# First experts of a small transformer tower: the second weights held in the array, 416 columns of hidden values moving

## Chip, cores and metric

The program runs on one core of a Trainium2 chip. The metric is the device time of one execution in microseconds (us), smaller is better. Times of the kernel before are the median of three runs and one execution taken with the hardware profiler. The engines are PE (matrix products), DVE (vector), ACT (activations), POOL (GpSimd) and SP (it issues the DMAs).

## What is computed

Four blocks of a transformer on 64 short sequences of 26 tokens, 1664 tokens of 192 values, all in fp32. The change is in the feed-forward part of the first block, where every token goes through all 32 experts:

```python
def _L0_ffn_ref(x, gate_w, gate_b, w1, b1, w2, b2):
    C = 192; E = 32; H = 4 * C
    gates = jax.nn.softmax(x @ gate_w + gate_b, axis=-1)
    h = jax.nn.gelu(jnp.einsum('btc,ech->bteh', x, w1) + b1, approximate=False)
    y = jnp.einsum('bteh,ehc->btec', h, w2) + b2
    out = jnp.einsum('bte,btec->btc', gates, y)
    return out
```

The result is added to the tokens `h` (`h = h + ffn(layernorm(h))`), and the next block begins with a layer norm of the sum.

## The kernel before

The 1664 tokens are 13 tiles of 128 (`TILES`), in four blocks of 3, 3, 3 and 4 tiles (`BLOCKS`, L33), so 384, 384, 384 and 512 tokens. The hidden size 768 is six chunks of 128 (`HC`). Products run in the fp32r type. To keep precision each operand is divided into a high part (the value cast to fp32r) and a low part (the value less its high part), and a product is made of several.

**Up products.** `up(e, j, k)` (L845) makes the six hidden chunks of block k: `five` (L590) issues five products a chunk, with 128 columns of the first weights stationary and the block's 384 or 512 normalised tokens moving. The chunk has channels down and tokens along. It lands in one of four PSUM banks (4 to 7). ACT applies GELU into one of three `hid` buffers (L905), DVE casts it to `hid_hi` (L936) and subtracts to get `hid_lo` (L939).

**Down products.** `down(e, j, k)` (L858) takes the tiles of a block one by one. The stationary operand is the hidden tile, 128 channels by 128 tokens. Moving is `w2[j]`, whose row holds 192 columns of high and 192 of low part, and each chunk has two products:

```python
nc.tensor.matmul(o[:, 0:2 * D], hid_hi[k % 2][:, m, c], w2[j][:, m, :],
                 start=m == 0, stop=False)
ins = nc.tensor.matmul(o[:, 0:D], hid_lo[k % 2][:, m, c], w2[j][:, m, 0:D],
                       start=False, stop=m == HC - 1)
```

The result has tokens down and the 192 outputs along (high part of the weights in the first 192 columns of the bank, low part in the second). `gather` (L954) on DVE multiplies each half with the tile's gate, a value per token and so per partition, and adds it to `h_tok` in one operation (L962, L968). Four banks (0 to 3) take the tiles in turn. The second biases, weighted with the gates, are 13 products of the turned gates (`gate_t`, 32 x 1664) with the biases (L842), added by L921.

**Order.** Each engine has its own order written out, tied by semaphores. On PE an expert is `up(0), up(1), down(0), up(2), down(1), up(3), down(2), down(3)`; on DVE it is `split(0), split(1), gather(0), split(2), gather(1), split(3), gather(2), gather(3)`. Two experts are the body of a hardware loop. In expert 0, `logits` comes ahead, the turning of the gates stands after `up(0)`, the second biases after `up(1)`. In the last expert DVE adds statistics (L389) and means (L393) of each finished tile, which the next phase's root needs all of.

**Weights.** SP loads an expert's 1344 KB into `raw[j]` two experts ahead (L808). POOL divides them in `split_weights` (L756): the high parts after half of the previous expert's splits, the low parts (L768, L771) after all of its 24 splits. PE waits for them at the head of an expert.

## Time and profile before

| | us |
|---|---|
| median of 3 runs | 2989.89 |
| lowest and highest | 2987.41, 2991.16 |
| the profiled execution | 2989.68 |
| its span in the trace | 2987.9 |

In 40 slices of the span, each digit the busy share in tenths (PEclk is the granted clock of PE in tenths of full speed):

```profile
PE   8889999999999999999999788797988889957678
PEld 7679999999999999999999687676566789945557
DVE  3867777777777777777777788523569567778876
ACT  2433233233333233333233344311555333334433
POOL 1312211211211211211211211021213101122550
PEclk9889999999999999999999899798989889978888
```

The first experts are the slices from the third to the twenty-second. PE's busy time is the union of its products' intervals, which overlap: a product's duration is longer than its distance to the next.

### The profile page before, as it was taken

The numbers are of one execution on the slowest core, as the hardware profiler recorded it, in microseconds if no ns is written. First come the engines' busy times: TensorE is split into PE (matmuls) and PEld (weight loads), VectorE is DVE, ScalarE is ACT, GpSimd is POOL, SyncE is SP. The second block draws the span as 40 slices with busy tenths as digits, with TensorE's granted clock in tenths as the row PEclk, the third lists the DMA queues.
The fourth block names the chain that finished last, engine by engine and source line by source line (L and its number), as shares of the span: only waits on it lengthen the run. The fifth ranks groups of instructions, "written<-read, shape, count | busy, mean of one in ns | idle before, by whom it ended". The sixth has DMA issues, their size and how long they took to land. (4 is left out here: it accounts for less than half of the span.)

```text
span 2987.9 us, 57872 instructions
## 1 busy us (share of the span) xinstructions
PE 2719.2 (91%) x20693; PEld 2465.2 (83%) x20693; DVE 2088.5 (70%) x5299; ACT 1061.3 (36%) x2060; POOL 620.7 (21%) x807
## 2 busy tenths in 40 slices
PE   8889999999999999999999788797988889957678
PEld 7679999999999999999999687676566789945557
DVE  3867777777777777777777788523569567778876
ACT  2433233233333233333233344311555333334433
POOL 1312211211211211211211211021213101122550
PEclk9889999999999999999999899798989889978888
DMA  3001001011011011010001000085000100000000
GB/s 141 20 38 38 21 36 37 19 37 37 19 37 37 19 37 37 19 37 37 19 19 40 2 2 2 17 251 155 1 12 4 54 19 19 1 11 17 25 20 18
DMA packets 24466, 105.65 MB, mean 35 GB/s; under 512 B 4455, under 2 KB 9463, under 8 KB 19086
## 3 DMA queue, kind: packets, MB, share of 16 engines
q1 hardware_dynamic: 22654, 99.62, 9.6%
q0 software_dynamic: 1584, 3.30, 0.3%
q8 instruction: 105, 1.72, 0.2%
q14 instruction: 123, 1.01, 0.1%
HBM read 98.32 MB, written 6.64 MB: 35 GB/s over the span
## 5 line engine op out<-in xcount | busy, mean ns | idle before, releaser
L905 ACT ACTIVATE hid<-bank,dat 128x384 f32<-128x384 f32 (+1 forms) x912 | 554.4, 608 | 1144.1 <-PE bank L595 1032.3
L870 PE MATMUL bank<-w,hid_hi 128*128 128x384 f32 x2964 | 858.5, 361 | 2.2 <-DVE y_tok L921 1.6
L872 PE MATMUL bank<-w,hid_lo 128*128 128x192 f32 x2964 | 745.5, 252 | 0.0
L872 PEld LDWEIGHTS bank<-w,hid_lo 128*128 128x128 f32 x2964 | 570.7, 193 | 1.7
L870 PEld LDWEIGHTS bank<-w,hid_hi 128*128 128x128 f32 x2964 | 561.3, 189 | 5.7 <-issue 4.1
L939 DVE TENSOR_TENSOR hid_lo<-hid,hid_hi 128x384 fp32r<-128x384 f32 (+1 forms) x912 | 539.8, 592 | 31.5
L936 DVE CAST hid_hi<-hid 128x384 fp32r<-128x384 f32 (+1 forms) x912 | 341.0, 374 | 126.6 <-ACT hid L905 125.2
L962 DVE SCALAR_TENSOR_TENSOR h_tok<-bank,gate,h_tok 128x192 f32<-128x192 f32 x416 | 173.5, 417 | 246.8 <-PE bank L872 243.4
L595 PE MATMUL bank<-xa_hi,w_hi 128*128 128x384 f32 (+1 forms) x912 | 324.5, 356 | 8.3 <-DVE w_lo L748 5.1
L595 PE MATMUL bank<-xa_lo,w_hi 128*128 128x384 f32 (+1 forms) x912 | 323.0, 354 | 0.0
L595 PE MATMUL bank<-xb,w_lo 128*128 128x384 f32 (+1 forms) x912 | 322.4, 353 | 0.0
L595 PE MATMUL bank<-xa_hi,w_lo 128*128 128x384 f32 (+1 forms) x912 | 321.7, 353 | 0.0
L595 PE MATMUL bank<-xb,w_hi 128*128 128x384 f32 (+1 forms) x912 | 320.2, 351 | 0.0
L768 POOL TENSOR_TENSOR w_lo<-raw,w_hi 128x1536 fp32r<-128x1536 f32 x36 | 125.6, 3490 | 675.6 <-DVE hid_lo L939 675.6
L1632 POOL COPY n_tok<-p_x 32x312 f32<-32x312 f32 (+1 forms) x192 | 94.3, 491 | 476.0 <-DVE p_x L2198 330.5
L595 PEld LDWEIGHTS bank<-xa_hi,w_hi 128*128 128x128 f32 x912 | 172.6, 189 | 18.3 <-issue 5.7
L968 DVE SCALAR_TENSOR_TENSOR h_tok<-bank,gate,h_tok 128x192 f32<-128x192 f32 x416 | 173.7, 418 | 14.5
L595 PEld LDWEIGHTS bank<-xb,w_hi 128*128 128x128 f32 x912 | 172.6, 189 | 10.6
L763 POOL CAST w_hi<-raw 128x1536 fp32r<-128x1536 f32 x36 | 52.8, 1466 | 618.1 <-DVE hid_lo L939 564.6
L595 PEld LDWEIGHTS bank<-xa_hi,w_lo 128*128 128x128 f32 x912 | 172.5, 189 | 9.9
L595 PEld LDWEIGHTS bank<-xb,w_lo 128*128 128x128 f32 x912 | 172.3, 189 | 9.8
L595 PEld LDWEIGHTS bank<-xa_lo,w_hi 128*128 128x128 f32 x912 | 172.9, 190 | 8.5
(359 smaller groups left out, 4286.2 us busy)
## 6 DMA issues: line engine op xcount, KB each, us to landing
raw<-in_L_exp SPq DMA_DIRECT2D x36, 1344.0 KB, 5.7
w_e<-in_L_exp SPq DMA_DIRECT2D x20, 576.0 KB, 4.0
w_e<-in_L_exp SPq DMA_DIRECT2D x20, 384.0 KB
pix<-in_pixels SPq DMA_DIRECT2D x6, 832.0 KB, 10.4
w_e<-in_L_exp SPq DMA_DIRECT2D x20, 195.0 KB
raw<-in_L_mlp SPq DMA_DIRECT2D x2, 1344.0 KB, 5.6
wp_raw<-in_L_att SPq DMA_DIRECT2D x1, 2304.0 KB, 8.3
route_rows<-in_rows_clear SPq DMA_DIRECT2D x1, 2000.0 KB, 23.0
```

The source lines that it names most:

```text
L595: ins = nc.tensor.matmul(o, l, r, start=start and n == 0, stop=stop and n == 4)
L763: nc.gpsimd.tensor_copy(w1_hi[j][:, :, :], r1).then_inc(s["w_split"].sem, 1)
L768: nc.gpsimd.tensor_tensor(w1_lo[j][:, :, :], r1, w1_hi[j][:, :, :].bitcast(F32), ALU.subtract).then_inc(s["w_split"].sem, 1)
L870: nc.tensor.matmul(o[:, 0:2 * D], hid_hi[k % 2][:, m, c], w2[j][:, m, :], start=m == 0, stop=False)
L872: ins = nc.tensor.matmul(o[:, 0:D], hid_lo[k % 2][:, m, c], w2[j][:, m, 0:D], start=False, stop=m == HC - 1)
L905: nc.scalar.activation(hid[(6 * k + m) % 3][:, 0:128 * nt], bank[4 + (6 * k + m) % 4][:, 0:128 * nt], func, bias=bias).then_inc(s["h_act"] ...
L936: nc.vector.tensor_copy(hid_hi[k % 2][:, m, 0:w], h).then_inc(s["dve_step"].sem, 1)
L939: nc.vector.tensor_tensor(hid_lo[k % 2][:, m, 0:w], h, hid_hi[k % 2][:, m, 0:w].bitcast(F32), ALU.subtract).then_inc(s["h_split"].sem, 1)
L962: nc.vector.scalar_tensor_tensor(res[:, t, :], o[:, 0:D], g, res[:, t, :], ALU.mult, ALU.add).then_inc(s["dve_step"].sem, 1)
L968: nc.vector.scalar_tensor_tensor(res[:, t, :], o[:, D:2 * D], g, res[:, t, :], ALU.mult, ALU.add).then_inc(s["y_used"].sem, 1)
L1632: nc.gpsimd.tensor_copy(p_bd[t % 2][r, :, SLOT * im:SLOT * im + SLOT], p_x[t % 2][r, 0:H, 0:SLOT]).then_inc(s["bd_low"].sem, 1)
```

## The change

For the first experts alone `turned_experts_phase` stands in place of `experts_phase`.

- Tokens are taken in four equal spans of 416 (`SPANS`), for the up products, ACT and the splits too.
- The down products have the second weights stationary and `hid_hi` or `hid_lo` of a span moving, 416 columns. Part 0 makes outputs 0 to 127 with three products a chunk (high x high, high x low, low x high). Part 1 makes outputs 128 to 191 with two: its stationary operand `both` holds 64 columns of high and 64 of low part, so that the upper 64 partitions of the result are the share of the weights' low part. So 18 + 12 = 30 products a span.
- The result has outputs down and tokens along. The gate is then a value per column. The 32 x 1664 turned gates are written to DRAM, and for each expert and span one row of 416 is read back into all 128 partitions of `gate_b`. DVE multiplies with it into `y_new` and adds `y_new` to the sums `y_sum`, which lie in `y_tok` (part 0) and `n_tok` (part 1): four operations a span.
- The second biases are 8 products of 416 columns, copied into the sums.
- In the last expert PE turns the finished sums back, tile by tile: a transpose of part 0 and a product of part 1 with `fold`, a 128 x 64 table that adds partitions p and p + 64. DVE adds the result to `h_tok` and takes statistics and means.
- POOL's low part of the second weights is two operations (768 and 384 elements) in place of one of 1152, its high part likewise.
- SP's loop over the experts is written out, with the gate rows' DMAs between the weights'. On PE and DVE the last two experts stand outside the loop (on DVE they did before).

The diff, cut to its core:

```diff
+SPANS = [(416 * k, 416) for k in range(4)]
+DONE = [(0, 3), (3, 3), (6, 3), (9, 4)]
...
+        y_new = [sb(f"y_new{j}", [128, 416], scope=ex) for j in range(2)]
...
+        gate_b = sb("gate_b", [128, TOK], scope=ex)
...
+        def turned_w2(j):
+            flat = w2[j][:, :, :].rearrange("p c n -> p (c n)")
+            return [flat[:, HC * 128 * y:HC * 128 * (y + 1)].rearrange("p (c n) -> p c n", c=HC) for y in range(3)]
+        def split_turned(pool, b, e, j, i, before_low=None):
...
+            a_hi, a_lo, both = turned_w2(j)
+            nc.gpsimd.tensor_copy(w1_hi[j][:, :, :], r1).then_inc(s["w_split"].sem, 1)
+            nc.gpsimd.tensor_copy(a_hi, ra).then_inc(s["w_split"].sem, 1)
+            nc.gpsimd.tensor_copy(both[:, :, 0:DB], rb).then_inc(s["w_split"].sem, 1)
+            if before_low:
+                before_low()
+            pool.wait_ge(s["w_split"].sem, b["w_split"] + 6 * e + 1)
+            nc.gpsimd.tensor_tensor(w1_lo[j][:, :, :], r1, w1_hi[j][:, :, :].bitcast(F32),
+                                    ALU.subtract).then_inc(s["w_split"].sem, 1)
+            pool.wait_ge(s["w_split"].sem, b["w_split"] + 6 * e + 3)
+            nc.gpsimd.tensor_tensor(a_lo, ra, a_hi.bitcast(F32), ALU.subtract).then_inc(s["w_split"].sem, 1)
+            nc.gpsimd.tensor_tensor(both[:, :, DB:2 * DB], rb, both[:, :, 0:DB].bitcast(F32),
+                                    ALU.subtract).then_inc(s["w_split"].sem, 1)
...
+            def sync(sp):
+                def gate_rows(e, k):
+                    c0, n = SPANS[k]
+                    line = gates_d[e:e + 1, c0:c0 + n]
+                    sp.dma_start(gate_b[:, c0:c0 + n], bass.AP(line.tensor, line.offset, [[0, 128], [1, n]]))                        .then_inc(gate_in[k], 16)
+                sp.wait_ge(s["t_used"].sem, gating["kept"])
+                sp.dma_start(gates_d[:, :], gate_t[0:E, :]).then_inc(gate_out, 16)
+                sp.wait_ge(gate_out, 16)
+                for k in range(4):
+                    gate_rows(0, k)
+                for e in range(E):
+                    if e + 2 < E:
+                        sp.wait_ge(s["w_split"].sem, b["w_split"] + 6 * (e + 1))
+                        sp.dma_start(raw[e % 2][:, :], dram[e + 2]).then_inc(w_in[e % 2].sem, 16)
+                    for k in range(4):
+                        if e + 1 < E:
+                            sp.wait_ge(s["y_used"].sem, b["y_used"] + down_unit(e, k) + 2)
+                            gate_rows(e + 1, k)
...
+                def second_biases():
+                    gating["tensor"][2](pe)
+                    w = dat[0:E, DATA_COLS[b2_col]]
+                    for u in range(8):
+                        c0, n = SPANS[u // 2]
+                        if u >= 4:
+                            pe.wait_ge(s["y_used"].sem, b["y_used"] + u - 3)
+                        nc.tensor.matmul(bank[u % 4][:, 0:n], w[:, 128 * (u % 2):128 * (u % 2) + 128],
+                                         gate_t[0:E, c0:c0 + n], start=True, stop=True).then_inc(s["y_full"].sem, 1)
...
+                def down(e, j, k):
+                    n = SPANS[k][1]
+                    a_hi, a_lo, both = turned_w2(j)
+                    u = down_unit(e, k)
+                    pe.wait_ge(s["h_split"].sem, b["h_split"] + 24 * e + 6 * k + 6)
+                    for part in range(2):
+                        pe.wait_ge(s["y_used"].sem, b["y_used"] + u + part - 3)
+                        o = bank[(down_unit(0, k) + part if not is_last(e) else u + part) % 4][:, 0:n]
+                        for m in range(HC):
+                            hi, lo = hid_hi[k % 2][:, m, 0:n], hid_lo[k % 2][:, m, 0:n]
+                            steps = ((a_hi, hi), (a_hi, lo), (a_lo, hi)) if part == 0 else ((both, hi), (both, lo))
+                            for y, (w, x) in enumerate(steps):
+                                ins = nc.tensor.matmul(o, w[:, m, :], x, start=m == 0 and y == 0,
+                                                       stop=m == HC - 1 and y == len(steps) - 1)
+                        ins.then_inc(s["y_full"].sem, 1)
+                def back(k):
+                    t0, nt = DONE[k]
+                    pe.wait_ge(s["dve_step"].sem, b["dve_step"] + added(E - 1, k))
+                    for part in range(2):
+                        u = back_unit(k) + part
+                        pe.wait_ge(s["y_used"].sem, b["y_used"] + u - 3)
+                        for y, t in enumerate(range(t0 + 2 * part, min(t0 + 2 * part + 2, t0 + nt))):
+                            o, c = bank[u % 4][:, D * y:D * y + D], slice(128 * t, 128 * t + 128)
+                            nc.tensor.transpose(o[:, 0:DA], y_sum[0][:, c], shp[:, SHAPE_COLS["ident"]])
+                            ins = nc.tensor.matmul(o[:, DA:D], y_sum[1][:, c], shp[:, SHAPE_COLS["fold"]], start=True,
+                                                   stop=True)
+                        ins.then_inc(s["y_full"].sem, 1)
+                def body(e, j, i):
+                    pe.wait_ge(s["w_split"].sem, b["w_split"] + 6 * (e + 1) - (2 if is_first(e) else 0))
+                    up(e, j, 0)
+                    if is_first(e):
+                        gating["tensor"][1](pe)
+                    for k in range(1, 4):
+                        up(e, j, k)
+                        if is_first(e) and k == 1:
+                            second_biases()
+                            pe.wait_ge(s["w_split"].sem, b["w_split"] + 6)
+                        down(e, j, k - 1)
+                        if is_last(e) and k > 1:
+                            back(k - 2)
+                    down(e, j, 3)
+                    if is_last(e):
+                        back(2)
+                        back(3)
+                over_experts(pe, body, 1)
...
+                def keep_second_biases():
+                    for u in range(8):
+                        c0, n = SPANS[u // 2]
+                        dve.wait_ge(s["y_full"].sem, b["y_full"] + u + 1)
+                        nc.vector.tensor_copy(y_sum[u % 2][:, c0:c0 + n], bank[u % 4][:, 0:n]).then_inc(s["y_used"].sem, 1)
...
+                def gather(e, j, k):
+                    c0, n = SPANS[k]
+                    c = slice(c0, c0 + n)
+                    u = down_unit(e, k)
+                    dve.wait_ge(gate_in[k], 16 * (e + 1))
+                    if not (is_first(e) and k == 0):
+                        dve.wait_ge(s["dve_step"].sem, b["dve_step"] + (added(e, k - 1) if k else STEPS * e))
+                    for part in range(2):
+                        dve.wait_ge(s["y_full"].sem, b["y_full"] + u + part + 1)
+                        o = bank[(down_unit(0, k) + part if not is_last(e) else u + part) % 4][:, 0:n]
+                        nc.vector.tensor_tensor(y_new[part][:, 0:n], o, gate_b[:, c], ALU.mult)                            .then_inc(s["y_used"].sem, 1)
+                    for part in range(2):
+                        dve.wait_ge(s["y_used"].sem, b["y_used"] + u + part + 1)
+                        nc.vector.tensor_tensor(y_sum[part][:, c], y_sum[part][:, c], y_new[part][:, 0:n], ALU.add)                            .then_inc(s["dve_step"].sem, 1)
+                def add_back(k):
+                    t0, nt = DONE[k]
+                    for part in range(2):
+                        u = back_unit(k) + part
+                        m = min(2, nt - 2 * part)
+                        t = t0 + 2 * part
+                        dve.wait_ge(s["y_full"].sem, b["y_full"] + u + 1)
+                        nc.vector.tensor_tensor(res[:, t:t + m, :], bank[u % 4][:, 0:D * m].rearrange("p (t d) -> p t d", d=D),
+                                                res[:, t:t + m, :], ALU.add).then_inc(s["y_used"].sem, 1)
+                        for y in range(t, t + m):
+                            statistics(dve, res, y, s["y_used"].sem, b["y_used"] + u + 1)
+                    for y in range(t0, t0 + nt):
+                        mean_of(dve, y, before)
+                def body(e, j, i):
+                    split(e, j, 0)
+                    for k in range(1, 4):
+                        split(e, j, k)
+                        if is_first(e) and k == 1:
+                            keep_second_biases()
+                        gather(e, j, k - 1)
+                        if is_last(e) and k > 1:
+                            add_back(k - 2)
+                    gather(e, j, 3)
+                    if is_last(e):
+                        add_back(2)
+                        add_back(3)
+                over_experts(dve, body, 1)
...
-        experts_phase(32, a["L0_exp"], "L0_b1", "L0_b2", h_tok, ACT.Gelu, w, g, stats_of=h_tok)
+        turned_experts_phase(32, a["L0_exp"], "L0_b1", "L0_b2", h_tok, ACT.Gelu, w, g)
...
+    o[p, SHAPE_COLS.lo("fold") + p % 64] = 1
...
-    col("L0_b2", g["L0_ffn_b2"])
+    col("L0_b2", np.pad(g["L0_ffn_b2"], ((0, 0), (0, 256 - D))))
...
-        "L0_exp": expert_pack(g["L0_ffn_w1"], g["L0_ffn_w2"]),
+        "L0_exp": turned_pack(g["L0_ffn_w1"], g["L0_ffn_w2"]),
```

On PE, in the first expert: the second biases and the first down products before. `w_0` is the second weights' buffer 0, `dat` holds the biases and `feat` the turned gates.

```order
L595 MATMUL bank<-xb,w_lo 128x384
L842 MATMUL bank<-dat,feat 128x192 x13
L870 MATMUL bank<-w_0,hid_hi 128x384
L872 MATMUL bank<-w_0,hid_lo 128x192
L870 MATMUL bank<-w_0,hid_hi 128x384
```

And the same place now, with the first five of the 30 down products of the span:

```order
L602 MATMUL bank<-xb,w_lo 128x416
L892 MATMUL bank<-feat,dat 128x416 x8
L919 MATMUL bank<-hid_hi,w_0 128x416
L919 MATMUL bank<-hid_lo,w_0 128x416
L919 MATMUL bank<-hid_hi,w_0 128x416 x2
L919 MATMUL bank<-hid_lo,w_0 128x416
```

The 36 products of three tiles, of 384 and 192 columns in turn, have become 30 of 416 for a span.

On DVE, the gather behind the second split of the first expert, before:

```order
L939 TENSOR_TENSOR hid_lo<-hid,hid_hi 128x384
L921 TENSOR_TENSOR h_tok<-bank,h_tok 128x192 x13
L962 SCALAR_TENSOR_TENSOR h_tok<-bank,gate,h_tok 128x192
L968 SCALAR_TENSOR_TENSOR h_tok<-bank,gate,h_tok 128x192
L962 SCALAR_TENSOR_TENSOR h_tok<-bank,gate,h_tok 128x192
```

And now:

```order
L981 COPY n_tok<-bank 128x416
L1008 TENSOR_TENSOR y_new<-bank,gate_b 128x416 x2
L1011 TENSOR_TENSOR y_tok<-y_tok,y_new 128x416
L1011 TENSOR_TENSOR n_tok<-n_tok,y_new 128x416
L992 CAST hid_hi<-hid 128x416
L994 TENSOR_TENSOR hid_lo<-hid,hid_hi 128x416
```

Six operations that read a bank and one tile are now two that read a bank and the gates, and two that read two tiles of SBUF.

On PE, the last expert, behind the third span's up products and the second's down products:

```order
L919 MATMUL bank<-hid_lo,w_1 128x416
L932 MATMUL bank<-shp,y_tok 128x128
L933 MATMUL bank<-shp,n_tok 128x64
L932 MATMUL bank<-shp,y_tok 128x128
L933 MATMUL bank<-shp,n_tok 128x64
L932 MATMUL bank<-shp,y_tok 128x128
L933 MATMUL bank<-shp,n_tok 128x64
L602 MATMUL bank<-xa_hi,w_hi 128x416
```

These turns of three tiles stand there once more a span later, and seven tiles are turned after the last down product.

## Rows read from the trace of the kernel before

**Rows 1.** The page's part 1, busy time by engine.
```profile
PE 2719.2 (91%) x20693; PEld 2465.2 (83%) x20693; DVE 2088.5 (70%) x5299; ACT 1061.3 (36%) x2060; POOL 620.7 (21%) x807
```

**Rows 2.** Windows: start:end length, busy us (instructions) by engine, PEclk, DMA share, GB/s.
```profile
240.00:1580.00 1340.00, 1340.00 (x8238) 1299.72 (x8237) 974.11 (x2213) 438.08 (x720) 256.61 (x119) 1.00 0.08 30
197.80:204.80 7.00, 5.93 (x27) 5.14 (x27) 5.73 (x18) 0.58 (x1) 2.55 (x2) 0.78 0.00 0
```

**Rows 3.** PE's timeline, two experts: start us, us, line, output<-inputs.
```profile
1003.86 0.36 PE L595 MATMUL bank<-xa_hi,w_hi 128*128 128x384 f32 x1
...
1009.12 0.34 PE L595 MATMUL bank<-xa_hi,w_hi 128*128 128x384 f32 x1
...
1029.82 0.42 PE L595 MATMUL bank<-xa_hi,w_hi 128*128 128x512 f32 x1
...
1036.80 0.34 PE L870 MATMUL bank<-w,hid_hi 128*128 128x384 f32 x1
...
1048.64 0.25 PE L872 MATMUL bank<-w,hid_lo 128*128 128x192 f32 x1
1048.72 0.36 PE L595 MATMUL bank<-xa_hi,w_hi 128*128 128x384 f32 x1
```

**Rows 4.** PE's timeline, query and key projections of the first attention.
```profile
60.15 0.35 PE L595 MATMUL bank<-xa_lo,wp_hi 128*96 128x416 f32 x1
...
61.66 0.35 PE L595 MATMUL bank<-xb,wp_lo 128*96 128x416 f32 x1
```

**Rows 5.** PE's timeline: turns, clock-keeping products, second biases of the first experts.
```profile
171.11 0.27 PE L447 MATMUL bank<-shp,n_tok 128*128 128x128 f32 x1
171.22 0.27 PE L408 MATMUL bank<-shp,n_tok 128*128 128x128 f32 x1
...
172.75 3.04 PE L403 MATMUL bank<-shp 128*128 128x428 f32 x8
...
197.79 1.56 PE L842 MATMUL bank<-dat,feat 32*128 32x192 f32 x8
199.89 4.38 PE L842 MATMUL bank<-dat,feat 32*128 32x192 f32 x18 [0.54 <-DVE h_tok L921]
```

**Rows 6.** DVE's timeline, last gather and last mean of the first experts.
```profile
1632.35 0.42 DVE L962 SCALAR_TENSOR_TENSOR h_tok<-bank,gate,h_tok 128x192 f32<-128x192 f32 x1 [0.62 <-PE bank L872]
...
1633.39 0.36 DVE L389 BATCH_NORM_STATS2 stats<-h_tok 128x6 f32<-128x192 f32 x1
1633.79 0.18 DVE L393 BATCH_NORM_AGGREGATE mv<-stats 128x2 f32<-128x6 f32 x1
```

**Rows 7.** Groups by form, 240 to 1580 us: count, busy us, mean ns, idle before.
```profile
L905 ACT ACTIVATE hid<-bank,dat 128x384 f32<-128x384 f32 x540 | 314.3, 582 | 666.3 <-PE bank L595 575.3 <-DVE hid_lo L939 89.2
L939 DVE TENSOR_TENSOR hid_lo<-hid,hid_hi 128x384 fp32r<-128x384 f32 x540 | 301.5, 558 | 18.7
L936 DVE CAST hid_hi<-hid 128x384 fp32r<-128x384 f32 x540 | 192.4, 356 | 69.4 <-ACT hid L905 69.3
...
L962 DVE SCALAR_TENSOR_TENSOR h_tok<-bank,gate,h_tok 128x192 f32<-128x192 f32 x386 | 161.0, 417 | 225.3 <-PE bank L872 221.9
...
L939 DVE TENSOR_TENSOR hid_lo<-hid,hid_hi 128x512 fp32r<-128x512 f32 x180 | 124.6, 692 | 6.2
```

**Rows 8.** DVE's timeline: first splits of an expert, last split of it.
```profile
1007.78 0.36 DVE L936 CAST hid_hi<-hid 128x384 fp32r<-128x384 f32 x1 [2.74 <-ACT hid L905]
...
1008.65 0.35 DVE L936 CAST hid_hi<-hid 128x384 fp32r<-128x384 f32 x1
...
1038.30 0.69 DVE L939 TENSOR_TENSOR hid_lo<-hid,hid_hi 128x512 fp32r<-128x512 f32 x1
```

**Rows 9.** POOL's timeline, low parts of the next expert's weights.
```profile
1039.25 3.49 POOL L768 TENSOR_TENSOR w_lo<-raw,w_hi 128x1536 fp32r<-128x1536 f32 x1 [18.25 <-DVE hid_lo L939]
1042.70 2.67 POOL L771 TENSOR_TENSOR w<-raw,w 128x1152 fp32r<-128x1152 f32 x1
```

**Rows 10.** The page's part 6, DMA issues: KB each, median us from issue to landing.
```profile
raw<-in_L_exp SPq DMA_DIRECT2D x36, 1344.0 KB, 5.7
```

118 lines of the change are left out of this document (109 added, 9 removed).

## The prediction

> **What bounds the kernel now.** First the shares of busy time [rows 1]: PE 91%, DVE 70%, ACT 36%. A share is a mean over stages, so next the stretch that the change touches [rows 2]: from 240 to 1580 us PE is busy 1340.00 of 1340.00 us at granted clock 1.00 (2.4 GHz), DVE 974 us (73%), ACT 438 (33%). The first experts are bound by PE, and their time is the number of products times the distance from one start to the next. Durations don't give it (they overlap); the timeline does [rows 3]. From 1003.86 to 1009.12 there are 30 up products of 384 columns: 175.3 ns each. From 1029.82 to 1036.80, 30 of 512: 232.7 ns. From 1036.80 to 1048.72, seven tiles of 12 down products, 42 pairs of 384 and 192 columns: 283.8 ns a pair. One expert is 1003.86 to 1048.72, 44.86 us, and the parts give it: 90 x 0.1753 + 30 x 0.2327 + 78 x 0.2838 = 44.9.
>
> **What a 192-column product really costs.** A pair less its 384-column half is 283.8 - 175.3 = 108.5 ns. At the rate of the longer products (0.45 ns a column) 192 columns would be 86. So 22 ns a pair, 78 x 22 = 1.7 us an expert, is overhead that the change can win, because all its products have 416 columns. Against that stands the number of columns. Before, a tile is 6 x (384 + 192) = 3456 columns and 13 tiles are 44928. Now a span is 6 x 5 x 416 = 12480 and four are 49920: 11% more, since the product of low part and low part is computed too.
>
> **The steady state, priced.** Between 384 and 512 columns the slope is (232.7 - 175.3)/128 = 0.448 ns, so 416 columns are 175.3 + 32 x 0.448 = 189.7 ns. The order shows 30 down products for each span, so an expert is 120 up and 120 down: 240 x 0.1897 = 45.52 us, 0.66 more than 44.86; over 32 experts **+21.1 us**. The nearest row of the very width, 128x416 with 96 weight columns [rows 4], is (61.66 - 60.15)/8 = 188.8 ns, which would make +14. I take the interpolation, as it has 128 weight columns, and keep +14 as the lower end.
> The Trainium skill (TensorE: Matmul & The Clock Gate, Back-to-back issue gap and LDWEIGHTS) has N/2.4 + 2.5 ns for a product of N columns and 107 ns for a load of 128. By it both versions of an expert would cost the same, 42.1 and 42.2 us, and the whole sum below would be about 3000 us. The trace disagrees (175.3 ns, not 162.5), and the measurement decides.
>
> **Second biases.** Before, 13 products of 192 columns; in fp32 each is two passes, 26 records over the 7 us before the first down product [rows 2, 5], part of it at half clock (0.78 granted) and with two waits of 0.54 us. Now 8 products, 16 passes of 416. From the clock-keeping products (428 columns, 3.04/8 = 0.38 us a pass) I price passes by their columns: 0.37 x 16 = 5.9 us against 0.17 x 26 = 4.4. That is +1.5, less 1.1 for the two waits: **+0.5 us**, rounded up. If the clock should stay up there, -2; if it falls longer, +2. The copies that free the banks are covered by these longer products.
>
> **Turning the sums back.** In the last expert PE turns 13 tiles: a transpose of 128 columns, 0.11 us [rows 5], and an fp32 product against "fold", two passes, bounded by two such: 0.33 us a tile. Six tiles stand between down products: **+2.0 us**. The other seven are in the tail.
>
> **The tail.** Before, PE's last product ends about 1632.3, the last gather starts 1632.35 and the last mean is ready at 1633.79 + 0.18, 1.65 us later [rows 6]. Only then can the next phase take its root. Now, after the last down product: DVE multiplies part 1 and adds twice, three operations of 416 elements. Nearest rows are the 384 and 512 forms of the split, 0.558 and 0.692 us [rows 7], so 0.59 each and, overlapped, 1.7 us in all. Meanwhile PE has turned tiles 6 to 8, and DVE adds them back (0.56 + 0.36), with three statistics (0.36, one under the next) and three means (0.18): about 2.3 us. PE turns the last four beside that. Then DVE adds these (2 x 0.56), four statistics, four means: 2.9 us. Sum 6.9 us against 1.65: **+5.2 us**, bounds +4 and +7.
>
> **What is costed at nothing, and its cover.** *DVE.* An expert has 24 split pairs. At 384 columns they follow each other at 0.87 us [rows 8]; 32 columns more on both operations make about 0.92, under PE's group of five, 0.948. The 26 gathers of 0.417 us become 8 products and 8 sums of 0.6: 9.6 for 10.8 us. DVE stays near 33 of 45.5 us. Its order puts the gather of a span behind the next split, and it ends 1.7 us into the up products at the head of an expert, where it ended at 1.2 (1007.78 - 2.74 against 1003.86). Every second expert a gap of some 2.7 us follows (the loop's turn; ACT's tile had been ready) [rows 7, 8]. So the first split would start at 4.4 us, end at 5.3, and the ACT tile that waits for its buffer (0.58 at 384 columns) end at about 6.1; PE needs it for its eighth group, at 7 x 0.948 = 6.6. Slack 0.5. *GpSimd.* Low parts start 0.26 us after the last split of the expert, which ends 2.19 us behind the up products (1038.99 against 1036.80), and take 3.49 + 2.67 [rows 3, 8, 9]. Three operations instead of two, priced by the line through 1536 and 1152 elements, are 3.49 + 1.86 + 1.04 = 6.4: end at 2.15 + 6.4 = 8.5 us of the 11.4 that the two last spans of down products give. Slack 2.8. *Gates.* Write and four broadcasts follow the turned gates, ready before 197.79 [rows 5]. Two transfers at the 5.7 us of a 1344 KB load [rows 10] end by 209.2; the first gather would want them at about 209. Banks for two spans stand between DVE and PE, so even 10 us late costs nothing. Later rows land a whole expert early, and the next weights, queued behind them on SP, are wanted half an expert later.
>
> **Sum.** 21.1 + 0.5 + 2.0 + 5.2 = 28.8 us on the profiled execution's 2989.7, which is within 0.2 of the median: **3018 us**, 1.0% slower.
>
> **Rivals.**
> *B, a column a cycle, faster.* The down products now stream the hidden values. If they took 416/2.4 = 173.3 ns, as the granted clock allows, an expert would be 120 x 0.1897 + 120 x 0.1733 = 43.56: -1.30 x 32 = -41.6, with the other 7.7 us 2956. It decides from a down product below 182 ns, where an expert costs 0.24 less than now and the 7.7 are paid. For it: every product of the stretch is over its cycles, and the cause may lie in the up operand. Against it: 384 and 512 columns, and 416 elsewhere [rows 4], all show 0.45 ns a column, with other operands. Chance 0.05.
> The skill's N/2.4 + 2.5 (same page and section), applied to the down products alone, would give 175.8 ns and about 2966 us.
> *C, PE waits at each expert, slower still.* DVE's new sums read two SBUF tiles, where the old gather read PSUM and one [rows 7]; those of the third span fall beside GpSimd's low parts of 3.5 us [rows 9]. If the two exclude one another, GpSimd ends later by up to 4 x 0.6 = 2.4 us, still inside 2.8; or DVE is held for 3.5 us and breaks the 0.5 of slack at the loop's turn. A wait of 1 to 2 us an expert gives 32 to 64 more: 3050 to 3082. Against it: in their place the sums come 2 us and more before the next up products. Chance 0.07.
> The skill (SBUF — State Buffer, SBUF: two separate sides) says just this: GpSimd and a DVE operation with two SBUF inputs share a port pair that one holds for the whole instruction. No row here shows such a collision, because the order keeps the low parts behind the splits.
> *D, within 0.2%.* Down products near 182 ns, 2984 to 2996. Chance 0.04. That the change does not do what it says I set aside: the order shows its products.
>
> **Numbers.** The forecast has 0.84. Its own ends: -7 for the price of rows 4, -2 biases, -1 tail, and 4 either way for where the clock falls in the phases behind, which all shift; +2 biases, +2 tail, +5 for 0.3 us at 15 loop turns. Most of these don't meet, so 3003 to 3032, which leaves out the rivals. Within 0.2% (6 us) is about what a measurement of this kernel cannot tell from no change. Faster 0.05 (B), same 0.04 (D), slower 0.91 (forecast and C).
>
> **What would show it.** An expert of 45.5 us with PE busy throughout; down products 190 ns apart; an expert of 43.6 is B, idle time before the first up product is C. The last mean 7 us behind the last down product. Wrong would be: any idle time of PE between 240 and 1580 us, or a distance under 186 ns.

## The result and the profile after

The changed kernel is slower, by a little under half of what was forecast.

| | us |
|---|---|
| before, median of 5 runs | 2989.89 |
| after, median of 5 runs | 3002.61 (2998.00 to 3007.09) |
| ratio after to before, as recorded over all runs | 1.0052, interval 1.0039 to 1.0064 (the two medians alone give 1.0043) |
| after, the profiled execution | 3003.47 (before 2989.68) |
| its span | 3001.7 (before 2987.9) |

The forecast was 3018 us, in 3003 to 3032. The direction was right, the median lies 15 us under it and just outside the low end. The same kernel was run again later (after_again), beside the kernel before: 1.0042 (1.0028 to 1.0056). In the changed kernel the lines stand lower: `five` is L602, the clock-keeping products L410, ACT's GELU L968, the down products L919.

The windows view of the steady stretch (columns as in [rows 2]):

```profile
240.00:1600.00 1360.00, 1360.00 (x7204) 1348.56 (x7203) 975.94 (x1922) 438.07 (x720) 279.73 (x180) 1.00 0.16 48
```

PE is again busy for the whole stretch at granted clock 1.00, so it is still the bound, and what counts is again products times distance. That takes PE's timeline (start us, us, line, output<-inputs), which answers to [rows 3]:

```profile
1001.32 0.35 PE L919 MATMUL bank<-hid_hi,w 128*128 128x416 f32 x1
...
1012.62 0.35 PE L602 MATMUL bank<-xa_hi,w_hi 128*128 128x416 f32 x1
...
1023.98 0.35 PE L919 MATMUL bank<-hid_hi,w 128*128 128x416 f32 x1
...
1057.94 0.35 PE L602 MATMUL bank<-xa_hi,w_hi 128*128 128x416 f32 x1
```

From 1001.32 to 1012.62 there are 60 down products, 188.3 ns each; from 1012.62 to 1023.98, 60 up products, 189.3 ns. One expert is 1012.62 to 1057.94: 45.32 us against 44.86. Over 32 experts that is 14.7 us.

The first expert, after and then before (the first and last row of the biases, and the first down product):

```profile
199.17 6.93 PE L892 MATMUL bank<-feat,dat 32*128 32x416 f32 x16
206.03 0.71 PE L919 MATMUL bank<-hid_hi,w 128*128 128x416 f32 x1
```

```profile
204.81 0.66 PE L870 MATMUL bank<-w,hid_hi 128*128 128x384 f32 x1 [0.54 <-DVE h_tok L921]
```

The biases take 6.86 us to the first down product; before they took 204.81 - 197.79 = 7.02 [rows 5].

The end of the first experts: PE's last down product and the next phase's first turn, then DVE's tail, which answers to [rows 6].

```profile
1648.73 0.35 PE L919 MATMUL bank<-hid_lo,w 128*128 128x416 f32 x1
...
1657.38 0.45 PE L454 MATMUL bank<-shp,n_tok 128*128 128x128 f32 x1 [5.26 <-ACT n_tok L477]
```

```profile
1649.11 0.59 DVE L1008 TENSOR_TENSOR y_new<-bank,gate_b 128x416 f32<-128x416 f32 x1 [1.57 <-PE bank L919]
...
1654.82 0.36 DVE L400 BATCH_NORM_AGGREGATE mv<-stats 128x2 f32<-128x6 f32 x4
```

The last down product ends at 1649.08, the last mean is ready at 1655.18: 6.1 us, against 1.65. The next phase's first turn stands at 1657.38, 21.2 us later than the 1636.16 of before. But the run ends only 13.8 us later by the profile, and 12.7 by the medians. So 7.4 us by the profile, 8.5 by the medians, come back behind the changed phase.

The groups by form on the same stretch (count, busy us, mean ns, idle before) answer to [rows 7]:

```profile
L994 DVE TENSOR_TENSOR hid_lo<-hid,hid_hi 128x416 fp32r<-128x416 f32 x720 | 426.7, 593 | 24.8
L992 DVE CAST hid_hi<-hid 128x416 fp32r<-128x416 f32 x720 | 270.7, 376 | 14.4 <-ACT hid L968 7.8
L1008 DVE TENSOR_TENSOR y_new<-bank,gate_b 128x416 f32<-128x416 f32 x241 | 142.7, 592 | 344.9 <-PE bank L919 341.1
L1011 DVE TENSOR_TENSOR y_tok<-y_tok,y_new 128x416 f32<-128x416 f32 x120 | 101.1, 842 | 0.0
L1011 DVE TENSOR_TENSOR n_tok<-n_tok,y_new 128x416 f32<-128x416 f32 x121 | 96.0, 793 | 0.0
```

The splits and the products with the gates have the durations forecast (0.38 and 0.59 us). The sums do not: 0.84 and 0.79 us on average for 0.59. The timelines of POOL and DVE show why:

```profile
1052.32 1.85 POOL L806 TENSOR_TENSOR w<-raw,w 128x768 fp32r<-128x768 f32 x1
1054.13 1.36 POOL L807 TENSOR_TENSOR w<-raw,w 128x384 fp32r<-128x384 f32 x1
```

```profile
1041.62 0.58 DVE L1011 TENSOR_TENSOR y_tok<-y_tok,y_new 128x416 f32<-128x416 f32 x1
...
1053.00 1.62 DVE L1011 TENSOR_TENSOR y_tok<-y_tok,y_new 128x416 f32<-128x416 f32 x1
1054.54 1.40 DVE L1011 TENSOR_TENSOR n_tok<-n_tok,y_new 128x416 f32<-128x416 f32 x1
```

A sum alone takes 0.58 us. The one that starts inside POOL's L806 ends at 1054.62, 0.45 us after L806 does (1054.17), and the next ends 0.45 us after L807 (1055.94 and 1055.49). Each waited for POOL's instruction and then ran. That is rival C's mechanism, and it costs DVE some 2 us an expert. PE does not see it: POOL is done at 1055.49, 2.45 us ahead of the next expert (forecast 2.8), and PE has no idle time. Nor did the turn of the loop: DVE's first splits of the two experts seen here start at 1014.64 and 1059.96, each after 0.23 us of waiting for ACT, and neither has a gap of 2.7 us as in [rows 8]. Over the whole stretch DVE's idle time ahead of these casts is 14.4 us, where it was 69.4 [rows 7].

The Trainium skill (SBUF — State Buffer, SBUF: two separate sides) says that GpSimd and a DVE operation with two SBUF inputs hold a shared pair of ports for a whole instruction. The trace agrees, with the 1.62 and 1.40 us above.

### The profile page after: what moved, and what is told of

It is laid out like the page before. It is cut to its first block and busy times, and to the rows that moved or that the text cites. A ratio compares the mean times of both kernels' runs of the same rounds, so it can differ in the third digit from the quotient of the medians.

```text
span 3001.7 us, 54449 instructions
## 1 busy us (share of the span) xinstructions
PE 2740.8 (91%) x19570; PEld 2510.7 (84%) x19570; DVE 2089.5 (70%) x4982; ACT 1061.9 (35%) x2060; POOL 641.8 (21%) x871
## 5 line engine op out<-in xcount | busy, mean ns | idle before, releaser
L968 ACT ACTIVATE hid<-bank,dat 128x416 f32<-128x416 f32 x768 | 467.1, 608 | 980.5 <-PE bank L602 929.3
L919 PE MATMUL bank<-hid_hi,w 128*128 128x416 f32 x2304 | 686.3, 352 | 0.0
L919 PE MATMUL bank<-hid_lo,w 128*128 128x416 f32 x1536 | 538.3, 350 | 0.0
L994 DVE TENSOR_TENSOR hid_lo<-hid,hid_hi 128x416 fp32r<-128x416 f32 x768 | 455.2, 593 | 26.5
L919 PEld LDWEIGHTS bank<-hid_hi,w 128*128 128x128 f32 x2304 | 433.2, 188 | 4.4 <-issue 1.2
L602 PE MATMUL bank<-xa_hi,w_hi 128*128 128x416 f32 (+2 forms) x912 | 321.9, 353 | 7.9 <-DVE w_lo L756 5.1
L602 PE MATMUL bank<-xb,w_lo 128*128 128x416 f32 (+2 forms) x912 | 322.5, 354 | 0.0
L602 PE MATMUL bank<-xa_lo,w_hi 128*128 128x416 f32 (+2 forms) x912 | 322.2, 353 | 0.0
L602 PE MATMUL bank<-xb,w_hi 128*128 128x416 f32 (+2 forms) x912 | 321.2, 352 | 0.0
L602 PE MATMUL bank<-xa_hi,w_lo 128*128 128x416 f32 (+2 forms) x912 | 320.5, 351 | 0.0
L992 DVE CAST hid_hi<-hid 128x416 fp32r<-128x416 f32 x768 | 288.6, 376 | 16.1 <-ACT hid L968 9.6
L919 PEld LDWEIGHTS bank<-hid_lo,w 128*128 128x128 f32 x1536 | 289.7, 189 | 2.1
L803 POOL TENSOR_TENSOR w_lo<-raw,w_hi 128x1536 fp32r<-128x1536 f32 x32 | 112.3, 3511 | 629.2 <-DVE hid_lo L994 629.2
L602 PEld LDWEIGHTS bank<-xa_hi,w_hi 128*128 128x128 f32 x912 | 172.1, 189 | 11.9 <-issue 5.7
L602 PEld LDWEIGHTS bank<-xa_lo,w_hi 128*128 128x128 f32 x912 | 172.4, 189 | 3.5
L602 PEld LDWEIGHTS bank<-xb,w_hi 128*128 128x128 f32 x912 | 172.3, 189 | 3.4
L602 PEld LDWEIGHTS bank<-xa_hi,w_lo 128*128 128x128 f32 x912 | 172.2, 189 | 2.4
L602 PEld LDWEIGHTS bank<-xb,w_lo 128*128 128x128 f32 x912 | 171.9, 188 | 2.6
```

Of the source, the lines that this page charges most:

```text
L602: ins = nc.tensor.matmul(o, l, r, start=start and n == 0, stop=stop and n == 4)
L803: nc.gpsimd.tensor_tensor(w1_lo[j][:, :, :], r1, w1_hi[j][:, :, :].bitcast(F32), ALU.subtract).then_inc(s["w_split"].sem, 1)
L919: ins = nc.tensor.matmul(o, w[:, m, :], x, start=m == 0 and y == 0, stop=m == HC - 1 and y == len(steps) - 1)
L968: nc.scalar.activation(hid[(6 * k + m) % 3][:, 0:n], bank[4 + (6 * k + m) % 4][:, 0:n], func, bias=dat[:, bass.ds(HC * e + col, 1)]).then_ ...
L992: nc.vector.tensor_copy(hid_hi[k % 2][:, m, 0:n], h).then_inc(s["dve_step"].sem, 1)
L994: nc.vector.tensor_tensor(hid_lo[k % 2][:, m, 0:n], h, hid_hi[k % 2][:, m, 0:n].bitcast(F32), ALU.subtract).then_inc(s["h_split"].sem, 1)
```

## The experiments

Twelve runs were made in three groups, each beside runs of the kernel before on the same chip (medians there: 2990.69 in the first group, 2987.08 in the second, 2987.40 in the third; the changes below are against these), with 2 (low288) to 12 executions each. The ratios are the recorded ones and differ a little from the quotients of the medians. "Expert" is the distance of one expert's first up product to the next's.

| run | expert, us | median, us | ratio to before, interval |
|---|---|---|---|
| low240 | 45.12 | 2996.54 | 1.0025 (1.0012 to 1.0037) |
| low288 | 46.63 | 3047.05 | 1.0186 (1.0159 to 1.0213) |
| delay | 44.87 | 2997.08 | 1.0024 (1.0012 to 1.0035) |
| early_low | 45.32 | 2998.40 | 1.0024 (1.0013 to 1.0035) |
| spans | 45.16 | 2995.56 | 1.0026 (1.0014 to 1.0038) |
| after_again | 45.32 | 3000.55 | 1.0042 (1.0028 to 1.0056) |
| low16 | 46.13 | 3027.73 | 1.0129 (1.0110 to 1.0147) |
| packed16 | 44.29 | 2963.57 | 0.9920 (0.9905 to 0.9935) |
| grouped16 | 43.92 | 2956.76 | 0.9898 (0.9882 to 0.9915) |
| low16_grouped | 43.50 (mean 43.59) | 2945.46 | 0.9859 (0.9842 to 0.9876) |
| wait5 | 44.87 | 2991.45 | 1.0012 (1.0002 to 1.0022) |
| wait20 | 44.87 | 3004.06 | 1.0061 (1.0048 to 1.0075) |

### What bounds a short product: low240, low288

The argument for the change was that a 192-column product takes 108.5 ns where 86 would do. These two widen it in the kernel before.

```diff
-                            ins = nc.tensor.matmul(o[:, 0:D], hid_lo[k % 2][:, m, c], w2[j][:, m, 0:D],
+                            w_lo = 240 if E == 32 else D
+                            ins = nc.tensor.matmul(o[:, 0:w_lo], hid_lo[k % 2][:, m, c], w2[j][:, m, 0:w_lo],
```

> The kernel before, in the first experts alone the product of hid_lo moves 240 columns instead of 192 (it adds a piece of low part times low part). Theory: a pair is bound by the weight load behind the short product, about 108.5 ns, and 240 columns at 0.4525 ns are 108.6 ns, so the pair stays at 284 ns, an expert at 44.9 us and the total at 2990 within 6 us. Rival (a fixed cost of 22 ns per short product, columns on top): pair 305 ns, 1.7 us more an expert, total about 3044 us.

> As low240 with 288 columns. Theory: past the cover of the load, 288 x 0.4525 = 130 ns, pair 305 ns, 1.7 us more an expert, total about 3044 us. Rival (fixed cost plus columns): pair 327 ns, 3.4 us more an expert, total about 3098 us.

PE's timeline, the first down product of the last block of an expert and the next up product, 42 pairs later, in low240 and then in low288:

```profile
1041.36 0.34 PE L870 MATMUL bank<-w,hid_hi 128*128 128x384 f32 x1
...
1053.40 0.34 PE L595 MATMUL bank<-xa_hi,w_hi 128*128 128x384 f32 x1
```

```profile
1023.29 0.34 PE L870 MATMUL bank<-w,hid_hi 128*128 128x384 f32 x1
...
1036.18 0.34 PE L595 MATMUL bank<-xa_hi,w_hi 128*128 128x384 f32 x1
```

With 48 more columns a pair goes from 283.8 to 286.7 ns (an expert from 44.87 to 45.12 us, over 78 pairs 3 ns each). With 96 more it is 306.9, an expert 46.63. So between 192 and 240 columns the low product costs 108 to 112 ns almost whatever its width, and from there to 288 columns its columns count. The rival, a fixed cost with the columns on top, is out. So the product of 192 columns was bound by something of fixed length. That this is the loading of 128 weight columns for the product behind it is argued here, as the part of the work that does not depend on the moving width; low16 and low16_grouped below speak for it too.
The Trainium skill (TensorE: Matmul & The Clock Gate, LDWEIGHTS) gives the load of P weight columns as P/1.2 ns, so 107 ns for 128; the 108.5 ns agree.
The gain of the change was therefore real: 22 ns a pair. It was eaten by its 11% more columns.

### The spans: spans

The changed kernel with the spans of the kernel before, so that in an expert only the form of the down products differs from the kernel before.

```diff
-SPANS = [(416 * k, 416) for k in range(4)]
+SPANS = [(0, 384), (384, 384), (768, 384), (1152, 512)]
```

> The changed kernel with spans of 384, 384, 384 and 512 columns instead of 416 each; the number of columns and of products is the same. Theory (a product costs its columns, 175.3 and 232.7 ns): 180 x 0.1753 + 60 x 0.2327 = 45.5 us an expert against the 45.3 measured with 416, so 6 us more, total 3003 to 3013 us. Rival (the down form is cheaper in itself than the up form): down products of 384 below 174 ns, total at or below the changed kernel's.

PE's timeline, the down products of the first span:

```profile
1019.96 0.33 PE L920 MATMUL bank<-hid_hi,w 128*128 128x384 f32 x1
...
1025.16 0.33 PE L603 MATMUL bank<-xa_hi,w_hi 128*128 128x384 f32 x1
```

30 down products in 5.20 us, 173.3 ns, where up products of the same width take 174.7 (5.24 us for the 30 from 1025.16 to the 1030.40 of the next down product). At 512 columns it is 228.0 ns (1047.79 to 1054.63) against 231.9 (1035.60 to 1042.56). So my theory missed, and its rival holds: the down form is cheaper in itself than the up form. The unequal spans make an expert of 45.16 us, less than the 45.32 of the equal ones and less than I expected. So widths of 384 and 512 are a little cheaper than four of 416: on the line from 384 (173.3) to 512 (228.0) 416 columns would be 187.0, and they are 188.3. The total, 8.5 us above before instead of 13.5, went along, though its interval overlaps after_again's.

### The order of GpSimd's work: early_low

The changed kernel, in which the low parts of the next weights follow the high parts at once.

```diff
-                    split_turned(pool, b, e + 1, j, i, before_low)
+                    split_turned(pool, b, e + 1, j, i)
```

> The changed kernel, but GpSimd's low parts of the next expert's weights don't wait for the 24th split: they follow the high parts at once, beside DVE's splits and sums that read two SBUF tiles. Theory (the two exclude one another): splits or sums are held for up to 3.5 us, GpSimd's operations are longer than 3.51 us in the mean, and PE may wait, up to 1 us an expert, total 3003 to 3035 us. Rival (they don't): DVE means stay 0.593 and 0.58 us, GpSimd's 3.51 us, total 3003 within 6 us.

The group of the sums, and the timelines of POOL and DVE:

```profile
L1011 DVE TENSOR_TENSOR y_tok<-y_tok,y_new 128x416 f32<-128x416 f32 x120 | 125.4, 1045 | 0.0
```

```profile
1030.18 3.50 POOL L803 TENSOR_TENSOR w_lo<-raw,w_hi 128x1536 fp32r<-128x1536 f32 x1
1033.65 2.20 POOL L806 TENSOR_TENSOR w<-raw,w 128x768 fp32r<-128x768 f32 x1
```

```profile
1031.74 2.40 DVE L1011 TENSOR_TENSOR y_tok<-y_tok,y_new 128x416 f32<-128x416 f32 x1
1034.06 2.24 DVE L1011 TENSOR_TENSOR n_tok<-n_tok,y_new 128x416 f32<-128x416 f32 x1
```

The collisions became longer: a sum of 2.40 us ends 0.46 us behind L803 (1034.14 and 1033.68), the next, which starts at 1034.06 during L806, takes 2.24. A cast, which reads one tile alone, is held too: in each expert one L992 takes 1.19 us for 0.38, from 1036.22 to 1037.41, while L807 runs until 1037.17. DVE's busy time from 240 to 1600 us goes from 975.94 to 1029.08 us, another 1.8 us an expert, and still an expert of PE is 45.32 us. The wait is real and covered; that disposes of rival C.

### Where the 7 to 8 us come back: delay, wait5, wait20

`delay` puts 112 products of 416 columns behind the last down product of the kernel before. `wait5` and `wait20` put 10 or 42 copies in a row on DVE ahead of its last statistics, so that PE stands idle instead.

```diff
+                if E == 32:
+                    for _ in range(112):
+                        nc.tensor.matmul(bank[4][:, 0:416], w1_hi[0][:, 0, 0:128], xa_hi[:, 0:416], start=True, stop=True)
```

```diff
+                        if E == 32:
+                            for q in range(10):
+                                if q:
+                                    dve.wait_ge(filler, q)
+                                nc.vector.tensor_copy(n_tok[:, 0:2, :], h_tok[:, 0:2, :]).then_inc(filler, 1)
+                            dve.wait_ge(filler, 10)
```

> The kernel before with 112 more products of 416 columns (21.1 us) on PE behind the last down product of the first experts; their result is not used. Nothing else is changed. DVE's tail runs beside them, the next phase's turns wait for them. Theory (the phases behind are shorter only because the clock's falls land elsewhere when all is shifted): the time from the next phase's first turn to the end, 1351.7 us before and 1344.3 us in the changed kernel, will again differ from 1351.7 by several us, and the total is between 3000 and 3012 us. Rival (it is something of the changed kernel itself, so not here): 1351.7 within 1.5 us and the total 3008 to 3010 us, as about 2 us of the 21 lie beside the old tail.

> The kernel before with ten copies of 384 elements in a row on DVE ahead of the last statistics of the first experts, about 0.40 us each, so that the last mean and all behind it come 4 us later; nothing else changes and PE stands idle meanwhile, as in the changed kernel's tail. Theory (the phases behind give time back when they are shifted, whatever shifts them, as in the run delay, where 21 us put in cost 6.4): between -4 and +2 us at the end. Rival (the give-back in delay was because PE was kept busy up to the next phase): +4 us.

> The same with 42 such copies, about 17 us. Theory (a shift alone changes what the granted clock does in the phases behind): the clock-keeping products of the next phase come 17 us later, the end only 3 to 9 us later, the difference lost again in the attention behind, where the granted clock reads higher. Rival (PE warm at the start of the next phase made the difference in delay): +17 us or more at the end, since a PE that stood idle also starts at half clock.

PE's timeline at the next phase's first turns, of delay and then of wait20:

```profile
1655.71 0.30 PE L447 MATMUL bank<-shp,n_tok 128*128 128x128 f32 x1 [2.17 <-ACT n_tok L470]
```

```profile
1655.65 0.45 PE L448 MATMUL bank<-shp,n_tok 128*128 128x128 f32 x1 [20.37 <-ACT n_tok L471]
```

Both reach this point together, 19.5 us later than before (1636.16; 3.0 of wait20's had already come about ahead of expert 1). They do not end together. delay costs 6.4 us at the end (2990.69 to 2997.08; by the ratio's interval 4 to 10), under what both its theory and its rival gave. wait20 costs 16.7 (2987.40 to 3004.06; 14 to 22) for the 16.5 put in, and wait5 4.1 (1 to 7) for 3.9. So by the medians a time in which PE stands idle is paid in full, and my theory, that any shift gives time back, is wrong. wait20 decides that; wait5 alone would not. A time that PE fills with products is paid by a third. Between delay and wait20 the difference is what PE does ahead of the next phase, as the rival said. It is not what happens in the changed kernel: there PE stands idle for 5.26 us ahead of its first turn, which takes 0.45 us as in wait20, and yet 7 to 8 us come back.

Where it is made is only partly seen. It is not at the head of the next phase. The first turn takes 0.30 us in delay and 0.45 in wait20, so PE came in at the upper clock in the one and at the lower in the other (granted clock from 1655.70 to 1657.00 us: 0.73 and 0.50); but the clock-keeping group behind the turns starts at the same time in both:

```profile
1661.66 3.04 PE L403 MATMUL bank<-shp 128*128 128x428 f32 x8
```

```profile
1661.76 3.04 PE L404 MATMUL bank<-shp 128*128 128x428 f32 x8
```

So the 10 us arise behind that. No trace shows them: delay's profiled execution (3004.88) is one of its dearer ones, 15.2 us above before's, and wait20's (3003.50) is only 13.8 above it. The difference rests on the medians. What the profiles of before and after show is a place. Each row is the stretch from the next phase's clock-keeping group to the following phase's (before, then after, then after_again; columns as in [rows 2]):

```profile
1643.40:1913.00 269.60, 219.77 (x3356) 199.30 (x3355) 216.03 (x759) 111.46 (x275) 47.49 (x95) 0.93 0.02 3
```

```profile
1663.60:1926.90 263.30, 215.91 (x3356) 195.97 (x3355) 216.32 (x760) 112.77 (x276) 48.31 (x95) 0.95 0.02 3
```

```profile
1665.10:1924.60 259.50, 214.52 (x3356) 194.55 (x3355) 216.94 (x760) 112.35 (x276) 48.51 (x95) 0.95 0.02 3
```

The same 3356 products of the second block take 269.6, 263.3 and 259.5 us, at granted clock 0.93, 0.95 and 0.95. In the profiles of the six kernels with the turned phase this stretch is 259.0 to 263.3 us, in the eight with the old form (before among them) 263.3 (low240) to 269.6; the two ranges touch. The granted clock does not order them alone: low16_grouped has 265.6 us at 0.93, low288 267.1 at 0.94. The medians go the same way. low16, low288, low240 and low16_grouped keep the old form, and their totals follow the expert alone: 32 x (46.13 - 44.87) = 40.3 for 40.7 measured, 56.3 for 56.4, 8.0 for 5.9, and with low16_grouped's mean expert of 43.59 us -41.0 for -41.9. The turned ones end below their own sums: after is 21.2 us late at the next phase and 12.7 at the end; packed16 is 11.8 us early at the clock-keeping group (1631.6 for 1643.4) and 23.5 at the end. Why the stretch is shorter behind the turned phase, and whether that is also what most of delay's executions had, stays open.

### Is the low part's type worth more than its form: low16, packed16, grouped16, low16_grouped

In these four the products with the low part of the hidden values take both operands in bf16, and so are rounded more coarsely. low16 is the kernel before with that; packed16 is the changed kernel with that, and with the low product of part 1 done as six products of 64 weight columns, alternately into the lower and the upper half of the result, which leaves out the low x low product.

```diff
-                            ins = nc.tensor.matmul(o[:, 0:D], hid_lo[k % 2][:, m, c], w2[j][:, m, 0:D],
+                            ins = nc.tensor.matmul(o[:, 0:D], h_low[k % 2][:, m, c], w2_low[j][:, m, 0:D],
```

```diff
-                            steps = ((a_hi, hi), (a_hi, lo), (a_lo, hi)) if part == 0 else ((both, hi), (both, lo))
+                            steps = ((a_hi, hi), (a_16[j], lo), (a_lo, hi)) if part == 0 else ((both, hi),)
...
+                        if part == 1:
+                            for m in range(HC):
+                                rows = slice(64 * (m % 2), 64 * (m % 2) + 64)
+                                ins = nc.tensor.matmul(o[rows, :], b_16[j][:, m, :], hid_lo16[k % 2][:, m, 0:n],
+                                                       start=False, stop=m >= HC - 2)
```

> The kernel before, in the first experts alone the product of hid_lo runs in bf16: DVE writes hid_lo as bf16 and GpSimd adds a bf16 copy of the second weights. The other product stays fp32r. Theory (the short product is bound by the load, and a bf16 load is no longer than a short product): pair 175 + 83 to 87 = 258 to 262 ns, 1.7 to 2.0 us less an expert, total 2925 to 2937 us. Rival (the bf16 load is as long): pair 284 ns, total 2990 us. A second rival: GpSimd's extra copy makes PE wait, total above 2990.

> The changed kernel with hid_lo and copies of the second weights in bf16 for the products of the low part; in part 1 these have 64 weight columns, and two chunks are computed side by side in the two halves of the array (partitions 0 to 63 and 64 to 127 of the bank, which are added at the end anyhow). Low part times low part falls away. Theory: a span is 18 x 0.188 + 6 x 0.176 + 3 x 0.18 = 5.0 us instead of 5.65, an expert 42.7 us instead of 45.3, total 2912 to 2925 us. Rival (the halves run one after the other): 5.5 us a span, total about 2985 us.

PE's timeline of low16, one pair, and of packed16: two chunks of part 0, and part 1's six small products.

```profile
1002.63 0.42 PE L880 MATMUL bank<-w,hid_hi 128*128 128x384 f32 x1
...
1002.93 0.42 PE L880 MATMUL bank<-w,hid_hi 128*128 128x384 f32 x1
```

```profile
1007.22 0.35 PE L927 MATMUL bank<-hid_lo,a 128*128 128x416 bf16 x1
...
1007.79 0.35 PE L927 MATMUL bank<-hid_lo,a 128*128 128x416 bf16 x1
...
1011.67 0.72 PE L932 MATMUL bank<-hid_lo,b 128*64 128x416 bf16 x6
1012.32 0.46 PE L608 MATMUL bank<-xa_hi,w_hi 128*128 128x416 f32 x1
```

Six products of 416 columns within 0.65 us, 108 ns each: the two halves ran side by side, as hoped. That is where packed16 gains. But both fell short of their theories. low16, expected at 258 to 262 ns a pair, made it longer, 300 ns from 1002.63 to 1002.93, and packed16, expected at an expert of 42.7 us, has 44.29: its chunk of three takes 0.57 us where three fp32r products take 0.565. It is not GpSimd's extra copies, low16's second rival: PE is busy 1340 of 1340 us from 240 to 1580 in low16, and all its experts take 46.13. Something in the mixture costs. Two further kernels change only the order of the products, so that the type changes once a tile or once in part 0:

```diff
+                        for m in range(HC):
+                            nc.tensor.matmul(o[:, 0:2 * D], hid_hi[k % 2][:, m, c], w2[j][:, m, :],
+                                             start=m == 0, stop=False)
                         for m in range(HC):
-                            nc.tensor.matmul(o[:, 0:2 * D], hid_hi[k % 2][:, m, c], w2[j][:, m, :],
-                                             start=m == 0, stop=False)
                             ins = nc.tensor.matmul(o[:, 0:D], h_low[k % 2][:, m, c], w2_low[j][:, m, 0:D],
```

> The kernel of packed16 (bf16 low parts, the 64-column products side by side) with part 0's 18 products of a span in another order: twelve fp32r first, then the six bf16, where one bf16 stood in each chunk between two fp32r. In packed16 a chunk of three takes 0.570 us; three fp32r would be 3 x 0.1882 = 0.565, and two fp32r with one bf16 product at 173.3 ns (416 columns at 2.4 GHz, worked out) 0.550. Theory (each change of type costs PE some 20 ns, beside a bf16 product that is faster): with one change instead of six, part 0 goes from 3.42 to about 3.32 us, an expert from 44.29 to about 43.9, the whole about 2951 us. Rival (no cost of the change of type, a bf16 product of 416 columns simply takes 193 ns): expert unchanged at 44.3, about 2963.

> The kernel of low16 (the kernel before with a bf16 low product of 192 columns) with the six fp32r products of a tile first and the six bf16 behind them. In low16 a pair took about 300 ns in the timeline, where the fp32r pair takes 283.8. Theory (a change of type costs, a bf16 product alone is shorter than 108 ns): a pair about 175.3 + 86 = 261 ns, expert 44.86 - 78 x 0.022 = 43.1, the whole about 2935 us. Rival 1 (the bf16 product is bound by its 128 weight columns like the fp32r one, 108 ns, and only the change of type goes away): pair about 286, expert 45.0, about 2993. Rival 2 (type changes cost nothing, the bf16 low product takes 125 ns): as low16, 3028.

PE's timeline of low16_grouped, one tile:

```profile
1003.70 1.32 PE L880 MATMUL bank<-w,hid_hi 128*128 128x384 f32 x6
1004.86 0.67 PE L883 MATMUL bank<-w,hid_lo 128*128 128x192 bf16 x6
1005.31 1.30 PE L880 MATMUL bank<-w,hid_hi 128*128 128x384 f32 x6
```

A tile takes 1.61 us, 268 ns a pair. Against low16 an expert loses 46.13 - 43.50 = 2.63 us for 13 x 5 = 65 changes there and back, 40 ns each; against packed16 grouped16 loses 0.37 us for 20, 18 ns each. In each of these comparisons only the order of the products differs, so the alternating order costs, at the granted clock of 1.00, and in low16 it costs more than the shorter product saves. The forecasts were near, with sizes off: low16_grouped was expected at 43.1 and 2935 us and is 43.50 and 2945.46, grouped16 expected at 2951 and is 2956.76.

But the order changes two things: how often the type changes, and whose weights are loaded behind a short product. PE's weight loads of the low product, before and in low16_grouped (count, busy us, mean ns, idle before; fp32r stands as f32):

```profile
L872 PEld LDWEIGHTS bank<-w,hid_lo 128*128 128x128 f32 x2319 | 442.7, 191 | 1.3
L883 PEld LDWEIGHTS bank<-w,hid_lo 128*128 128x128 bf16 x2382 | 176.4, 98 | 65.5 <-issue 65.5
```

A bf16 load lasts half as long as an fp32r one. In low16 an fp32r load stands behind each bf16 product, in low16_grouped behind one of six. If such a product still takes the 108.5 ns of before, then 300 - 175.3 - 108.5 = 16 ns are left for the change of type itself, near the 18 of the 416-column products, which at 176 ns and more (416 columns, bf16, in grouped16) are longer than those 108.5 in any order. So 16 to 18 ns for the change there and back, and the rest of the 40 for a load that is not covered, fits both pairs of kernels. It is worked out, and no run tells the two apart.

With one change a tile left, the bf16 product of 192 columns takes about 84 ns (265.9 a pair by the expert's time, less 175.3, less a sixth of 40): well under the 108 that bound the fp32r one. The Trainium skill (TensorE: Matmul & The Clock Gate, Weight-path perf modes) has a faster load for 128 weight columns of a type other than FP32; the 98 against 191 ns and the 84 ns agree with it.

Not all experts of low16_grouped are alike: most take 43.50 us, and of those that open the loop's body many take more, up to 43.88 (mean of 30 from 240.55 to 1548.11: 43.59). There PE starts a chunk up to 0.26 us late (at 813.57), behind an idle time of DVE of 3.45 us (to 811.80). The slack of 0.5 us that the prediction saw at the loop's turn is used up in this kernel.

low16_grouped beats both kernels, by 1.4% against before. It keeps the form of the kernel before, and the turned form with the same means (grouped16) is 11 us behind it.

## Why the forecast was right in direction and 15 us too high

- **PE stays the bound, no idle time.** Right. The forecast's test, idle time of PE between 240 and 1580 us, shows none.
- **The steady state, priced, +21.1 us.** The step that was mis-sized. It measured 14.7. The mechanism was right: 240 products of one width, 78 short products' overhead won, 11% more columns paid. But every 416-column product was taken as 189.7 ns, from up products of 384 and 512 columns, and it is 188.3 as a down product and 189.3 as an up product. The 1.4 ns on each of 3840 down products are 5.4 us, the 0.4 on as many up products 1.5. So the line between the widths was good to 0.4 ns for the form that it was read from, and what failed was to price the turned down products like up products: the spans run shows them 1.4 and 3.9 ns cheaper at 384 and 512 columns. The row of the very width [rows 4], 188.8 ns, which I kept as the low end because of its 96 weight columns, gave 14, but by luck: its products have the up form, and it lies between the two values. The distance did stay above the 186 ns that would have overturned the reasoning.
- **Second biases, +0.5.** Measured 6.86 for 7.02 us, so -0.2. A pass of 416 columns was longer than priced (0.43 for 0.37, at a granted clock of 0.84 from 199.17 to 206.03), and the waits went.
- **Turning back between down products, +2.0.** About 1.8 by the timeline: the last down product stands 16.8 us later, of which 14.5 had come by the last expert's start (1601.78 for 1587.28) and 0.5 is that expert's own.
- **The tail, +5.2.** Measured 6.1 for 1.65, so +4.45. Its parts fell as described; statistics and means overlap more.
- **Costed at nothing.** DVE, GpSimd and the gates' rows did cost PE nothing. GpSimd's slack was 2.45 for 2.8. The collision of rival C exists, and its cover held even when early_low made it twice as long.
- **The phases behind.** The sum ended at the first experts' end and gave what follows 4 us either way. Up to there it was 28.8 for 21.2 measured. Behind it the measured 21.2 became 12.7. This is half of the miss, and it is the term that I allowed too little for.
- **Rival B.** At 384 columns the down form takes 173.3 for 174.7 ns, a small part of what B wanted; 416 columns at 188.3 rule it out. **Rival D** needed 182.
- **The rule of the Trainium skill** (TensorE: Matmul & The Clock Gate, Back-to-back issue gap). N/2.4 + 2.5, which it gives for an isolated product, makes about 3000 us of the whole. That is near the result by luck: it makes an expert 42.2 us, and one takes 45.32.

So the total of 3002.6 is 14.7 (steady) - 0.2 + 1.8 + 4.45, which is 20.8, near the 21.2 at the next phase, less the 8.5 that came back. Of the 15 us that the forecast was too high, the part behind the first experts is not explained.

## What to carry to other kernels

Where an engine is busy without a gap, count its instructions and price each from a row of its own width and form. Where there is none for the new form, let the range hold a ns or two for it: on 3840 products they were 5 us here, and reading between widths within one form was off by no more. A short product is worth removing only if what replaces it costs less in columns than the short product wasted; here 22 ns a pair were won and 11% more columns cost more. A narrower type, in an order that changes type seldom, won what turning the operands round did not. And a shift of the phases behind need not cost its own length: compare one filled with the engine's work and one in which it is idle, by medians of many runs.

## What the runs showed that was not expected

- An fp32r product with 128 weight columns costs nearly the same at 192 and 240 columns, 108.5 and 111.4 ns (283.8 and 286.7 a pair). A bf16 one of 192 columns takes about 84.
- Down products with the hidden values moving are cheaper than up products of the same width: 173.3 for 174.7 ns at 384 columns, 228.0 for 231.9 at 512.
- Alternating fp32r and bf16 products costs PE 18 ns a change there and back at 416 columns and 40 with 192-column bf16 products, so it made low16's pair 16 ns dearer (300 for 283.8).
- Six bf16 products of 64 weight columns and 416 moving, alternately in the two halves, take 0.65 us.
- A DVE operation with two SBUF operands that meets a GpSimd operation waits for its end: 0.58 us became 1.62 and, in early_low, 2.40. A cast with one operand was held too, 1.19 us for 0.38.
- By the medians, time put in ahead of the next phase cost its length where PE was idle in it (16.5 us put in cost 16.7) and a third where PE worked (21.1 us cost 6.4). The cause is open.
- Single executions of one kernel spread over up to 15 us (delay 2992.97 to 3007.77), so a profile alone says little about a difference of 5 us behind the first experts.
